# Moving a cross-attention layer's key and value projections one layer earlier, through device memory

## The chip, the cores and the metric

The kernel runs on one core of a Trainium2 chip. The metric is the device time of one execution in microseconds (us). Before the change it is 2668.98 us, the median of three runs (2668.42 to 2671.52).

The core's engines work side by side: TensorE (PE) multiplies matrices out of the on-chip memory into eight accumulation banks, VectorE (DVE), ScalarE (ACT) and GpSimd (POOL) do elementwise work, and SyncE (SP) issues all the transfers of this kernel. [...]

## The reference, cut to what matters

Four attention layers run one after the other on 16 sequences of 128 rows by 512 columns. `ctx` is a second input of the same shape that no layer changes.

```python
x = L0(ctx, x, mask)          # latent attention, then an MLP
x = L1(x, ctx, mask)          # grouped attention (32 query heads, 8 key heads), no MLP
x = L2(x, ctx, mask)          # cross attention (16 heads), then an MLP
x = L3(ctx, x, mask)          # latent attention, then an MLP

def L1(hidden, enc, mask):
    q, k, v = hidden @ Wq + bq, enc @ Wk + bk, enc @ Wv + bv
    x = attention(q, k, v) @ Wo + bo + hidden
    return normalized(x) * gamma + beta

def L2(hidden, enc, mask):
    q = layer_norm(hidden) @ q_w + q_b
    k, v = enc @ k_w + k_b, enc @ v_w + v_b      # enc is ctx: they depend on no earlier layer
    hidden = attention(q, k, v) @ cproj_w + cproj_b + hidden
    return hidden + mlp(layer_norm(hidden))
```

## The kernel before

All four layers work on pairs of sequences, `p` from 0 to 7. Each matrix product is made in three passes (`three_passes`, L317): every operand is split into a rounded part and the rest, and high times high, high times low and low times high are summed. `ctx` is split once, in layer 0, and kept in device memory as `ctx_split`. Each later layer loads one pair of it (1 MB, `sp_c`, L1444) into the first half of each block of `XC`; the second half gets the layer's own input, turned by PE (`pe_turn_x`, L350) and split by ACT and DVE (`act_x`, `dve_x`). Weights come in 256 KB tiles: SP loads one into one of two buffers (`load_tile`, L296) and POOL splits it (`split_tile`, L304 to L308). SP loads tile n only when tile n-2 is split.

A pair runs in rounds: four in the grouped layer, two in the cross layer. A round is a chain. PE makes the scores (L317 with 32 rows), DVE takes the maxima (grouped: fused with the addition of the mask, L950; cross: L954), ACT the exponentials (L700), DVE the inverse sums (L972), POOL scales (`pool_norm`, L1274), PE turns the result (L453), ACT and DVE copy it out (L684, L959), and PE multiplies it with the values (`pe_attend`, L480). PE makes the scores of round k+1 before it turns round k. ACT and DVE then take the heads out (L714, L999), and after a sequence's last round comes the output projection (`pe_out`). DVE adds the residual (L1093) and takes the moments (L1078 to L1087), and POOL normalizes (`pool_root`, L1302 to L1309; in the grouped layer a second time for the next layer, `pool_again`, L1315). Scores, and the MLP's sums, use four of the eight banks. All other products share a ring of the other four (`begin`): a product can start when the bank used four products ago has been emptied.

The projections for pair p+1 stand between the rounds of pair p. In the grouped layer these are one small key block, two query blocks and one value block. In the cross layer they are two key blocks (`pe_keys`), two query blocks and two value blocks (`pe_values`); each key or query block is 24 matmuls of 256 columns, each value block 12 of 512. Keys and values go to `KT_C` and `V_C` by ACT (L730, L684) and DVE (L1017, L959), queries to `QT` (L738, L1026). Keys and queries stand together, after the first `pe_attend` of the pair, and the first key block waits until `dve_x` is done with pair p+1 (`aff_split`), although only the queries need it. The cross layer's 16 weight tiles are split by POOL in the grouped layer, two in each pair. The order on each engine is written out by hand in the functions named after it (`pe_gqa`, `act_gqa`, `dve_gqa`, `pool_gqa`, `sp_gqa` and so on for `cross`).

## Time and profile before

| | before |
|---|---|
| median of three runs | 2668.98 us |
| profiled execution | 2673.65 us, its span 2671.9 us |
| PE busy over the span | 93% (weight loads 78%) |
| DVE, ACT, POOL busy over the span | 46%, 41%, 41% |
| grouped layer, first key block to first cross projection | 802.45 to 1190.11 us |
| cross layer, from there to the first MLP product | 1190.11 to 1522.67 us |
| mean granted PE clock of the core | 0.97 of full |

A busy share over the whole span hides that the stages have different limits: in the MLPs PE never stops, in the grouped layer POOL is the busiest engine. The profiled execution is 4.7 us above the median of the three runs. [...]

### The profile page before, as it was taken

Reading aid. Unit: us, or ns where it says so; the run is one execution under the profiler, and the core shown is the slowest. Engines: PE = TensorE matmul, PEld = TensorE weight load, DVE = VectorE, ACT = ScalarE, POOL = GpSimd, SP = SyncE. Lnnn points to the kernel's source line nnn. Section 1 sums busy time; section 2 is a strip of 40 time slices with the busy share of each in tenths; the row PEclk is TensorE's granted clock in tenths of the full one; section 3 lists DMA queues with packets and bytes.
Section 4 is the critical chain, followed back from the end, with each engine's and each line's share of the span. In section 5 each row is a group of like instructions: output and inputs, shape, how many; then the busy total and the mean of one; then the engine's idle time right before and its main releaser. Section 6 shows DMA issues by size and latency. Waiting matters only on the chain.

```text
span 2671.9 us, 48698 instructions
## 1 busy us (share of the span) xinstructions
PE 2474.4 (93%) x18464; PEld 2072.0 (78%) x18464; DVE 1230.2 (46%) x3295; ACT 1086.5 (41%) x3705; POOL 1105.6 (41%) x1972
## 2 busy tenths in 40 slices
PE   7999998999997788857988899999899999899999
PEld 5887886888886666747877788888788888688887
DVE  4555564323225766644445533332355555432322
ACT  4555563111117777745556411111355555311111
POOL 2454446400035898963544560003244444640000
PEclk9999999999999999978999999999899999999999
DMA  4112212211112222221222231112211211321100
GB/s 155 57 57 70 90 49 92 63 48 48 56 61 85 82 92 83 66 84 64 72 96 92 76 122 48 48 40 61 78 49 49 89 48 49 98 63 41 48 32 16
DMA packets 110326, 181.30 MB, mean 68 GB/s; under 512 B 7888, under 2 KB 43408, under 8 KB 109072
## 3 DMA queue, kind: packets, MB, share of 16 engines
q1 hardware_dynamic: 110096, 178.19, 20.3%
q8 instruction: 149, 2.44, 0.4%
q14 instruction: 81, 0.66, 0.1%
HBM read 132.02 MB, written 46.14 MB: 67 GB/s over the span
## 4 chain that ended last, share of the span: by engine, by line
PE 80%; POOL 7%; ACT 6%; DVE 4%; issue 2%; DMA 1%; SPq 0%; DVEq 0%; POOLq 0%; ACTq 0%
PE banks L317 71%; PE banks L453 5%; ACT plain_high L700 4%; POOL plain_high L1274 4%; PE banks L480 3%; DVE neg_max L954 1%; PE banks L504 1%; DVE rounded_work L1052 1%; DVE plain_high L950 0%; POOL rounded_high L308 0%; POOL rounded_low L308 0%; PE banks L442 0%; DVE rounded_work L1026 0%; POOL rstd L1289 0%; ACT plain_high L684 0%
## 5 line engine op out<-in xcount | busy, mean ns | idle before, releaser
L317 PE MATMUL banks<-rounded_work,rounded_low 128*128 128x512 f32 (+1 forms) x2688 | 535.2, 357 | 58.3 <-issue 35.3
L1274 POOL TENSOR_SCALAR plain_high<-plain_high,inv_sum 128x128 f32<-128x128 f32 (+1 forms) x1024 | 386.7, 401 | 392.4 <-DVE inv_sum L972 391.3
L317 PEld LDWEIGHTS banks<-rounded_work,rounded_low 128*128 128x128 f32 x2688 | 447.4, 200 | 125.4 <-issue 53.6
L317 PE MATMUL banks<-rounded_work,rounded_high 128*128 128x512 f32 (+1 forms) x2400 | 488.2, 357 | 8.6 <-DMA rounded_work<-ctx_split 6.4
L929 ACT ACTIVATE plain_work<-banks,columns 128x512 f32<-128x512 f32 x192 | 132.5, 690 | 865.2 <-PE banks L317 865.2
L317 PEld LDWEIGHTS banks<-rounded_work,rounded_high 128*128 128x128 f32 x2400 | 399.1, 192 | 76.6 <-issue 9.4
L1250 DVE CAST rounded_work<-plain_work 128x512 fp32r<-128x512 f32 x192 | 102.0, 531 | 689.3 <-ACT plain_work L929 678.1
L317 PE MATMUL banks<-rounded_low,rounded_work 128*128 128x512 f32 x1728 | 413.1, 391 | 0.0
L317 PE MATMUL banks<-rounded_high,rounded_work 128*128 128x512 f32 (+1 forms) x1728 | 395.2, 381 | 0.0
L317 PEld LDWEIGHTS banks<-rounded_low,rounded_work 128*128 128x128 f32 x1728 | 322.1, 188 | 69.0 <-issue 3.0
L317 PEld LDWEIGHTS banks<-rounded_high,rounded_work 128*128 128x128 f32 x1728 | 314.1, 192 | 60.5 <-issue 1.4
L1412 POOL TENSOR_TENSOR plain_work<-plain_work 128x512 f32<-128x512 f32 x48 | 66.5, 1416 | 608.0 <-DMA plain_work<-x 417.4
L453 PE MATMUL banks<-ident,plain_high 128*128 128x128 f32 x1280 | 182.0, 289 | 59.8 <-POOL plain_high L1274 42.4
L700 ACT ACTIVATE plain_high<-plain_high,neg_max 128x128 f32<-128x128 f32 x512 | 198.0, 391 | 47.6 <-DVE neg_max L950 47.6
L954 DVE TENSOR_REDUCE neg_max<-banks 128x2 f32<-128x512 f32 (+1 forms) x320 | 204.5, 681 | 24.4 <-PE banks L442 24.4
L1274 POOL TENSOR_SCALAR plain_low<-plain_low,inv_sum 128x256 f32<-128x256 f32 x256 | 117.1, 479 | 237.4 <-DVE inv_sum L972 237.4
L453 PEld LDWEIGHTS banks<-ident,plain_high 128*128 128x128 f32 x1280 | 144.0, 146 | 90.2 <-issue 53.0
L700 ACT ACTIVATE plain_high<-banks,neg_max 128x256 f32<-128x256 f32 (+1 forms) x512 | 209.5, 462 | 7.4 <-DVE neg_max L954 7.4
L1252 DVE TENSOR_TENSOR rounded_work<-plain_work,rounded_work 128x512 fp32r<-128x512 f32 x192 | 159.1, 829 | 6.6
L972 DVE RECIPROCAL inv_sum<-row_sum 128x4 f32<-128x4 f32 (+1 forms) x224 | 41.4, 186 | 212.0 <-ACT plain_high L700 168.9
L317 PEld LDWEIGHTS banks<-rounded_work 32*128 32x128 f32 x3072 | 101.6, 188 | 43.0 <-issue 40.7
L317 PE MATMUL banks<-rounded_work 32*128 32x256 f32 (+1 forms) x3072 | 123.5, 292 | 10.2 <-DVE rounded_work L1026 8.1
(101 smaller groups left out, 3058.0 us busy)
## 6 DMA issues: line engine op xcount, KB each, us to landing
plain_work<-x SPq DMA_DIRECT2D x96, 256.0 KB, 2.8
plain_work<-mlp_w SPq DMA_DIRECT2D x96, 256.0 KB, 2.7
rounded_work<-ctx_split SPq DMA_DIRECT2D x24, 1024.0 KB, 5.9
u<-plain_work SPq DMA_DIRECT2D x48, 256.0 KB, 3.0
plain_work<-u SPq DMA_DIRECT2D x12, 1024.0 KB, 7.2
x<-plain_work SPq DMA_DIRECT2D x48, 256.0 KB, 2.2
plain_work<-attention_w SPq DMA_DIRECT2D x44, 256.0 KB, 2.7
plain_work<-inputs_t SPq DMA_DIRECT2D x8, 1024.0 KB, 7.8
```

What stands on the lines that cost most here:

```text
L317: mm = pe.matmul(dst, lhs(i), rhs(j), start=first and n == 0, stop=last and n == 2, skip_group_check=True)
L453: mm = pe.transpose(dst[:, t * P:(t + 1) * P], pr[:, r, t * P:(t + 1) * P], ident[:, :])
L480: mm = pe.matmul(dst[32 * r:32 * r + 32, i * P:(i + 1) * P], v, pt[:, r, at:at + P], start=t == 0, stop=t == n_t - 1, skip_group_check=True)
L504: mm = pe.transpose(dst[:, r * P:(r + 1) * P], u_nat[:, r, f * P:(f + 1) * P], ident[:, :])
L700: last = act.activation(pr[:, r, part], pr[:, r, part] if gqa else PS[:, r, part], ACT.Exp, scale=-1.0 if gqa else 1.0, bias=neg_max[:, R ...
L929: act.activation(gelu[:, j % 2, :], bank(key), ACT.Gelu_apprx_tanh, bias=col(y, 28 + j)).then_inc(evac_of(key), 1)
L954: dve.tensor_reduce(neg_max[:, R % 2, r, 0:y.segs], src.rearrange("p (g n) -> p g n", g=y.segs), AX.X, ALU.max, negate=True).then_inc(maxe ...
L972: dve.reciprocal(inv_sum[:, R % 2, 2 * half:2 * half + 2, 0:y.segs], row_sum[:, R % 2, 2 * half:2 * half + 2, 0:y.segs]).then_inc(inverted, 1)
L1250: dve.tensor_copy(G[:, j % 4, 0, :], gelu[:, j % 2, :]).then_inc(g_hi, 1)
L1252: dve.tensor_tensor(G[:, j % 4, 1, :], gelu[:, j % 2, :], G[:, j % 4, 0, :].bitcast(F32), ALU.subtract).then_inc(g_ready, 1)
L1274: last = pool.tensor_scalar(part, part, inv_sum[:, R % 2, r, g:g + 1], 1.0, ALU.mult, ALU.mult)
L1412: last = pool.tensor_tensor(res[:, r, :], res[:, r, :], wide_bias, ALU.add)
```

## The change

The cross layer's key and value projections move into the grouped layer. While `XC` holds the `ctx` half of pair p+1 for the grouped layer's own keys, PE also makes the two key and two value blocks of the cross layer from it. ACT and DVE put them into new buffers `k_ahead` and `v_ahead` (one of each), SP stores them in device memory (1 MB of keys and 512 KB of values for each pair), and the cross layer loads them back into two `KT_C` and two `V_C` buffers. The cross layer no longer loads `ctx_split`. Its input has its own buffer `XT_C`.

- PE, grouped layer: all four blocks of pair 0 stand ahead of the second scores. For each later pair, a key block stands after the first `pe_attend`, a key block after the second, a value block after the third and a value block at the end of the pair. Cross layer: keys and values are gone, and `pe_out` of the pair before moves from behind the queries to a place ahead of the first `pe_attend`; DVE's `dve_out` moves likewise.
- ACT and DVE follow. ACT waits for the stored keys or values of the pair before ahead of the next evacuation.
- SP: `ctx_split` for the grouped layer's pair p+1 is loaded when the cross layer's last value block of pair p is done (before: when the grouped layer's value block of pair p was). Key and value stores are added, and for pair 0 both stand ahead of the load for pair 1.
- POOL: of the cross layer's 16 tiles, the eight of keys and values are split in the last stretch of layer 0's MLP; four query tiles in pairs 0 to 3 of the grouped layer; four output tiles at the start of the cross layer.

PE in the grouped layer, before: one whole pair, from its second scores (L317 at 128x256 x24 from `rounded_work` alone; L453 turns, L350 turns the input, L480 attends, other L317 rows are projections).

```order
L317 MATMUL banks<-rounded_work 128x256 x24
L453 MATMUL banks<-ident,plain_high 128x128 x16
L350 MATMUL banks<-ident,plain_work 128x128 x8
L317 MATMUL banks<-rounded_high 128x512 x12
L480 MATMUL banks<-plain_work 32x128 x16
L317 MATMUL banks<-rounded_work,rounded_high 128x256 x12
L317 MATMUL banks<-rounded_work 128x256 x24
L453 MATMUL banks<-ident,plain_high 128x128 x16
L317 MATMUL banks<-rounded_work,rounded_high 128x256 x24
L480 MATMUL banks<-plain_work 32x128 x16
L317 MATMUL banks<-rounded_work 128x256 x24
```

The same stretch after the change:

```order
L324 MATMUL banks<-rounded_work 128x256 x24
L465 MATMUL banks<-ident,plain_high 128x128 x16
L359 MATMUL banks<-ident,plain_work 128x128 x8
L324 MATMUL banks<-rounded_high 128x512 x12
L495 MATMUL banks<-plain_work 32x128 x16
L324 MATMUL banks<-rounded_work,rounded_high 128x256 x12
L324 MATMUL banks<-rounded_work,rounded_low 128x256 x24
L324 MATMUL banks<-rounded_work 128x256 x24
L465 MATMUL banks<-ident,plain_high 128x128 x16
L324 MATMUL banks<-rounded_work,rounded_high 128x256 x24
L495 MATMUL banks<-plain_work 32x128 x16
L324 MATMUL banks<-rounded_work,rounded_low 128x256 x24
```

The two new rows `rounded_work,rounded_low 128x256 x24` are the cross layer's key blocks, each between an attend and the next scores.

PE in the cross layer, before: from a pair's second scores to those of the next pair.

```order
L317 MATMUL banks<-rounded_work 128x128 x48
L442 MATMUL banks<-plain_work,ones_row 128x512 x4
L453 MATMUL banks<-ident,plain_high 128x128 x16
L350 MATMUL banks<-ident,plain_work 128x128 x8
L480 MATMUL banks<-plain_high,plain_work 32x128 x16
L317 MATMUL banks<-rounded_work,rounded_low 128x256 x96
L317 MATMUL banks<-rounded_low,rounded_high 128x512 x12
L317 MATMUL banks<-rounded_work 128x128 x48
L442 MATMUL banks<-plain_work,ones_row 128x512 x4
L453 MATMUL banks<-ident,plain_high 128x128 x16
L317 MATMUL banks<-rounded_low,rounded_high 128x512 x12
L480 MATMUL banks<-plain_high,plain_work 32x128 x16
```

After:

```order
L324 MATMUL banks<-rounded_work 128x128 x48
L454 MATMUL banks<-plain_work,ones_row 128x512 x4
L465 MATMUL banks<-ident,plain_high 128x128 x16
L359 MATMUL banks<-ident,plain_work 128x128 x8
L324 MATMUL banks<-rounded_low,rounded_high 128x512 x12
L495 MATMUL banks<-plain_high,plain_work 32x128 x16
L324 MATMUL banks<-rounded_work,rounded_low 128x256 x48
L324 MATMUL banks<-rounded_work 128x128 x48
L454 MATMUL banks<-plain_work,ones_row 128x512 x4
L465 MATMUL banks<-ident,plain_high 128x128 x16
L324 MATMUL banks<-rounded_low,rounded_high 128x512 x12
L495 MATMUL banks<-plain_high,plain_work 32x128 x16
```

The 96 projection matmuls have become 48, the two value blocks that followed the last row are gone, and an output projection has moved from behind the queries to the place ahead of the attend.

The diff, cut to its core:

```diff
--- before.py
+++ after.py
-        KT_C = work(rounded, 16, 2, 4, 2 * P)
+        KT_C = [work(rounded, 16 - 8 * h, 2, 4, 2 * P) for h in range(2)]
+        XT_C = work(rounded, 0, 2, FB, 2 * P)
+        k_ahead, v_ahead = slots(rounded, 6, 2, 4, 2 * P), slots(plain, 7, 2, D)
...
         def pe_keys(pe, y, p, i):
-            if i == 0:
+            if i == 0 and y.kind != CROSS:
...
             if p == 0:
                 pe_weights(pe, y, "q")
+            if y.kind == CROSS and i == 0:
+                pe_inputs(pe, y, p)
+            x_t = XT_C if y.kind == CROSS else XC[:, :, :, 2 * P:4 * P]
...
+                pe.wait_ge(kt_loaded[p % 2], 16 * (p // 2 + 1))
                 for i in range(2):
-                    wait_evac(pe, ("K", y.n, p, i))
                     wait_evac(pe, ("Q", y.n, p, i))
...
+            if y.kind == CROSS:
+                pe.wait_ge(vc_loaded[p % 2], 16 * (p // 2 + 1))
...
             pe_scores(pe, y, 0, 0)
             pe_queries(pe, y, 0, 1)
             pe_values(pe, y, 0, 0)
+            for i in range(2):
+                pe_keys(pe, L[2], 0, i)
+            for i in range(2):
+                pe_values(pe, L[2], 0, i)
...
                 if more:
                     pe_keys(pe, y, p + 1, 0)
+                    pe_keys(pe, L[2], p + 1, 0)
                 pe_scores(pe, y, p, 2)
                 pe_turn_probs(pe, y, p, 1)
                 if more:
                     pe_queries(pe, y, p + 1, 0)
                 pe_attend(pe, y, p, 1)
+                if more:
+                    pe_keys(pe, L[2], p + 1, 1)
                 pe_scores(pe, y, p, 3)
                 pe_turn_probs(pe, y, p, 2)
                 if more:
                     pe_values(pe, y, p + 1, 0)
                 pe_attend(pe, y, p, 2)
                 if more:
+                    pe_values(pe, L[2], p + 1, 0)
                     pe_scores(pe, y, p + 1, 0)
                 pe_turn_probs(pe, y, p, 3)
                 pe_out(pe, y, 2 * p)
                 pe_attend(pe, y, p, 3)
                 if more:
                     pe_queries(pe, y, p + 1, 1)
+                    pe_values(pe, L[2], p + 1, 1)
             pe_out(pe, y, B - 1)
 
         def pe_cross(pe, y):
             pe_turn_x(pe, y, 0)
             for i in range(2):
-                pe_keys(pe, y, 0, i)
-            for i in range(2):
                 pe_queries(pe, y, 0, i)
             pe_scores(pe, y, 0, 0)
-            for i in range(2):
-                pe_values(pe, y, 0, i)
...
                     pe_turn_x(pe, y, p + 1)
+                if p:
+                    pe_out(pe, y, 2 * p - 1)
                 pe_attend(pe, y, p, 0)
                 if more:
-                    for i in range(2):
-                        pe_keys(pe, y, p + 1, i)
                     for i in range(2):
                         pe_queries(pe, y, p + 1, i)
                 else:
                     for f in range(FB):
                         pe_turn_u(pe, M[y.n], 0, f)
-                if p:
-                    pe_out(pe, y, 2 * p - 1)
                 if more:
                     pe_scores(pe, y, p + 1, 0)
                 pe_turn_probs(pe, y, p, 1)
                 pe_out(pe, y, 2 * p)
                 pe_attend(pe, y, p, 1)
-                if more:
-                    for i in range(2):
-                        pe_values(pe, y, p + 1, i)
             pe_out(pe, y, B - 1)
...
+                if p and i == 0:
+                    act.wait_ge(k_stored, 16 * p)
                 for j in range(2):
                     t = 2 * i + j
-                    last = act.activation(KT_C[:, 0, t, :], bank(key)[:, j * 256:j * 256 + 256], ACT.Identity, bias=col(y, 4 + t))
+                    last = act.activation(k_ahead[:, 0, t, :], bank(key)[:, j * 256:j * 256 + 256], ACT.Identity, bias=col(y, 4 + t))
                 last.then_inc(hi_done, hi_count(key))
 
...
+                if y.kind == CROSS:
+                    wait(act, v_stored, 16 * p)
+                act_copy(act, key, v_ahead[:, i, :] if y.kind == CROSS else V_L[p % 2][:, i, :])
 
...
-                split_tile(pool, ("a", 2), 2 * p)
+                if p < 4:
+                    split_tile(pool, ("qo", 2), p)
                 pool_norm(pool, y, p, 3)
-                split_tile(pool, ("a", 2), 2 * p + 1)
                 pool_bias(pool, y, 2 * p + 1)
...
         def pool_cross(pool, y):
+            pool.wait_ge(k_stored, 16 * PAIRS)
+            pool.wait_ge(v_stored, 16 * PAIRS)
+            split_tile(pool, ("qo", 2), 4)
+            split_tile(pool, ("qo", 2), 5)
             pool_norm(pool, y, 0, 0)
+            split_tile(pool, ("qo", 2), 6)
+            split_tile(pool, ("qo", 2), 7)
...
+                pool.wait_ge(down_done, base + 8)
+                for i in range(8):
+                    split_tile(pool, ("kv", 2), i)
                 pool.wait_ge(down_done, base + 11)
-                for i in range(8, 12):
-                    split_tile(pool, ("a", 1), i)
+                for i in range(4):
+                    split_tile(pool, ("o", 1), i)
...
+        def sp_keys_ahead(sp, p):
+            for i in range(2):
+                wait_evac(sp, ("K", 2, p, i))
+            sp.dma_start(keys_of[p], k_ahead.rearrange("p a b c -> p (a b c)").bitcast(F32)).then_inc(k_stored, 16)
+
+        def sp_values_ahead(sp, p):
+            for i in range(2):
+                wait_evac(sp, ("V", 2, p, i))
+            sp.dma_start(values_of[p], v_ahead.rearrange("p a b -> p (a b)")).then_inc(v_stored, 16)
+
+        def sp_ahead(sp, p):
+            sp_keys_ahead(sp, p)
+            sp_values_ahead(sp, p)
+
+        def sp_cross_keys(sp, p):
+            sp.dma_start(KT_C[p % 2].rearrange("p a b c -> p (a b c)").bitcast(F32), keys_of[p]).then_inc(kt_loaded[p % 2], 16)
+
+        def sp_cross_values(sp, p):
+            sp.dma_start(V_C[p % 2].rearrange("p a b -> p (a b)"), values_of[p]).then_inc(vc_loaded[p % 2], 16)
+
         def sp_gqa(sp, y):
             sp.wait_ge(s_filled[3], M[0].u0 + GROUPS)
...
+            sp_ahead(sp, 0)
             for p in range(PAIRS):
                 more, far = p + 1 < PAIRS, p + 2 < PAIRS
                 if more:
-                    wait_filled(sp, v_last(y, p))
+                    wait_filled(sp, ("V", 2, p, 1))
                     sp_c(sp, y, p + 1)
                     if p:
                         sp.wait_ge(s_free[3], y.use(p - 1, 3) + 1)
                     sp_qk_mask(sp, p + 1)
-                load_tile(sp, ("a", 2), 2 * p)
-                load_tile(sp, ("a", 2), 2 * p + 1)
+                if p < 4:
+                    load_tile(sp, ("qo", 2), p)
                 if p:
+                    sp_values_ahead(sp, p)
                     sp_store_h(sp, y, 2 * p - 2)
                 if far:
                     wait_filled(sp, ("X", y.n, p + 1, 1))
...
                     sp_store_h(sp, y, 2 * p - 1)
                     sp_store_u(sp, y, 2 * p - 1)
                     sp_next_hidden(sp, y, 2 * p + 1)
+                if more:
+                    sp_keys_ahead(sp, p + 1)
...
-            wait_filled(sp, ("Q", 1, PAIRS - 1, 1))
-            sp_c(sp, y, 0)
+            wait_filled(sp, ("V", 2, PAIRS - 1, 1))
             sp_x(sp, y, 0)
+            sp.wait_ge(k_stored, 16 * PAIRS)
+            sp.wait_ge(v_stored, 16 * PAIRS)
+            load_tile(sp, ("qo", 2), 4)
+            load_tile(sp, ("qo", 2), 5)
             sp_mask(sp, y, 0)
+            sp.wait_ge(s_filled[3], prev.use(PAIRS - 1, 3) + 1)
+            sp_cross_keys(sp, 0)
+            sp_cross_keys(sp, 1)
+            wait_filled(sp, ("O", prev.round(PAIRS - 1, 3)))
+            sp_cross_values(sp, 0)
+            sp_cross_values(sp, 1)
             sp.wait_ge(biased, prev.b0 + B)
             sp_wide(sp, "L2_xattn_cproj_b")
             sp_gqa_tail(sp, prev)
...
-                if more:
-                    wait_filled(sp, v_last(y, p))
-                    sp_c(sp, y, p + 1)
+                if p and more:
+                    sp.wait_ge(s_filled[3], y.use(p - 1, 1) + 1)
+                    sp_cross_keys(sp, p + 1)
+                    wait_filled(sp, ("O", y.round(p - 1, 1)))
+                    sp_cross_values(sp, p + 1)
```

## Rows read from the trace of the kernel before

**Rows 1.** Stretches of six grouped and six cross pairs: from:to, length, each engine's busy time, clock, DMA.
```profile
859.55:1129.63 270.08, 219.87 (x2429) 183.99 (x2425) 186.67 (x1068) 211.57 (x930) 240.94 (x517) 0.94 0.25 80
1254.87:1495.36 240.49, 212.18 (x2114) 188.85 (x2113) 121.44 (x288) 132.81 (x558) 113.42 (x254) 0.92 0.27 91
```

**Rows 2.** Timeline of PE, grouped layer: start us, length us, engine, line, operation [idle before].
```profile
816.92 1.00 PE L317 MATMUL banks<-rounded_work 32*128 32x256 f32 x24
...
859.55 3.14 PE L317 MATMUL banks<-rounded_work,rounded_high 128*128 128x256 f32 x24
862.62 1.00 PE L317 MATMUL banks<-rounded_work 32*128 32x256 f32 x24
...
996.12 1.00 PE L317 MATMUL banks<-rounded_work 32*128 32x256 f32 x24
...
1005.05 1.69 PE L317 MATMUL banks<-rounded_work,rounded_high 128*128 128x256 f32 x12
...
1034.68 4.36 PE L317 MATMUL banks<-rounded_high 128*128 128x512 f32 x12
...
1129.56 3.13 PE L317 MATMUL banks<-rounded_work,rounded_high 128*128 128x256 f32 x24
```

**Rows 3.** Timeline of POOL, grouped layer: first and last scaling of a run of three.
```profile
1004.53 5.57 POOL L1274 TENSOR_SCALAR plain_high<-plain_high,inv_sum 128x128 f32<-128x128 f32 x16 [2.69 <-DVE inv_sum L972]
...
1028.22 5.57 POOL L1274 TENSOR_SCALAR plain_high<-plain_high,inv_sum 128x128 f32<-128x128 f32 x16
```

**Rows 4.** Timeline of PE, cross layer: its first block, then one pair and a later value block.
```profile
1190.11 13.72 PE L317 MATMUL banks<-rounded_work,rounded_low 128*128 128x256 f32 x96 [11.08 <-issue]
1205.88 1.59 PE L317 MATMUL banks<-rounded_work 32*128 32x128 f32 x48 [2.04 <-DVE rounded_work L1026]
...
1289.06 5.73 PE L317 MATMUL banks<-rounded_low,rounded_work 128*128 128x512 f32 x24
1294.72 1.58 PE L317 MATMUL banks<-rounded_work 32*128 32x128 f32 x48
...
1305.10 14.19 PE L317 MATMUL banks<-rounded_work,rounded_low 128*128 128x256 f32 x96 [3.44 <-issue]
...
1489.70 5.73 PE L317 MATMUL banks<-rounded_low,rounded_work 128*128 128x512 f32 x24
```

**Rows 5.** Timeline of ACT, cross layer: evacuations of the first two key blocks.
```profile
1195.24 0.84 ACT L730 ACTIVATE rounded_work<-banks,columns 128x256 fp32r<-128x256 f32 x2 [13.71 <-PE banks L317]
1198.11 0.84 ACT L730 ACTIVATE rounded_work<-banks,columns 128x256 fp32r<-128x256 f32 x2 [2.03 <-PE banks L317]
```

**Rows 6.** Timeline of DVE, cross layer: maxima, inverse sums, heads, the split of the input.
```profile
1283.54 1.28 DVE L954 TENSOR_REDUCE neg_max<-banks 128x4 f32<-128x512 f32 x2
...
1290.83 0.20 DVE L972 RECIPROCAL inv_sum<-row_sum 128x8 f32<-128x8 f32 x1 [2.58 <-ACT plain_high L700]
...
1292.74 1.12 DVE L999 SCALAR_TENSOR_TENSOR rounded_high<-banks,columns,rounded_high 128x128 fp32r<-128x128 f32 x4
...
1296.54 1.29 DVE L954 TENSOR_REDUCE neg_max<-banks 128x4 f32<-128x512 f32 x2 [1.02 <-PE banks L442]
...
1304.31 0.69 DVE L1043 TENSOR_TENSOR rounded_work<-plain_work,rounded_work 128x512 fp32r<-128x512 f32 x1
```

**Rows 7.** Transfers of the six grouped pairs: issuing engine, count, KB each, us to landing.
```profile
rounded_work<-ctx_split SPq DMA_DIRECT2D x5, 1024.0 KB, 5.9
x<-plain_work SPq DMA_DIRECT2D x12, 256.0 KB, 2.2
```

**Rows 8.** Timeline, end of layer 0's MLP: POOL's first, ninth and last splits; SP's load.
```profile
736.47 0.40 POOL L306 CAST rounded_high<-plain_work 128x256 fp32r<-128x256 f32 x1 [6.79 <-PE banks L317]
...
779.99 0.61 POOL L306 CAST rounded_high<-plain_work 128x512 fp32r<-128x512 f32 x1 [24.79 <-PE banks L317]
...
787.37 1.28 POOL L308 TENSOR_TENSOR rounded_high<-plain_work,rounded_high 128x512 fp32r<-128x512 f32 x1
```
```profile
793.55 0.61 SPq L1444 DMA_DIRECT2D rounded_work<-ctx_split x1
```

95 lines of the change are left out of this document (54 added, 41 removed).

## Prediction

> **What bounds the kernel now.** I read the busy shares first, then the same by stage, then the timelines of the two layers that the change touches, and last the chain of waits through them. The page's 93% for PE is a mean over stages. In the MLPs it is 100%, and there the change alters nothing. In the two attention layers it is not [rows 1]: over six grouped pairs PE is busy 219.87 of 270.08 us, POOL 240.94; over six cross pairs PE is busy 212.18 of 240.49 us and no other engine more than 133. So the grouped layer hangs on POOL and has PE time to spare, and the cross layer hangs on PE.
>
> Grouped layer: query blocks of the same kind start at 859.55 and, six pairs later, at 1129.56 [rows 2], so a pair takes 45.0 us. The chain through it is POOL's: the scaling that starts at 1004.53 and the one that ends at 1033.8 enclose 29.3 us in which POOL hardly stops (scalings, normalizations, one tile's split) [rows 3]. The remaining 15.7 us go through PE's last turn, output projection, attend and second query block, then through evacuation, maxima and exponentials back to POOL.
>
> Cross layer: value blocks start at 1289.06 and, five pairs later, at 1489.70 [rows 4], so a pair takes 40.1 us. PE stands still for 3.44 us in each pair ahead of the 96 projection matmuls, because the keys wait with the queries for the split input, and hardly elsewhere.
>
> **What moves, block by block.** Two key blocks are evacuated 2.88 us apart at full clock [rows 5]; two value blocks take 5.66 us from their start to the next scores [rows 4]. Four blocks are 5.75 + 5.66 = 11.4 us of PE per pair, taken from the cross layer and given to the grouped one.
>
> **Grouped layer, pairs 1 to 6.** PE is busy 36.65 us per pair now, in part at half clock (1034.68: 12 matmuls in 4.36 us [rows 2]; the granted clock over the stretch is 0.94 [rows 1]). With 11.4 us more it is 48.05 us, above today's 45.0: PE becomes the bound, and I take 48.1 us. A second way gives the same. Laying the new row of work out at full clock gives 43.7 us of PE; three of the four blocks stand directly ahead of scores and delay a round's maxima, and the waits for turned or scaled rows that are left come to about 4.5 us. The ends: 45.0 if every block falls into a gap that POOL leaves, 56.4 if none does. POOL itself loses work: two tiles per pair become one in pairs 0 to 3 and none later. One split lies on its chain, 2.2 us by the last four at the end of the MLP (779.99 to 788.65 [rows 8]), but this frees nothing once PE is last. ACT gets 2.3 us and DVE 2.4 us more per pair, on 35 and 31 us busy of 45; that is room enough, except that each key block is evacuated ahead of the next maxima (0.9 us of delay per round, in the 48.1). Six pairs at +3.1: **+18.5 us** (0 to +68).
>
> **Grouped layer, pair 0 and pair 7.** All four blocks stand ahead of the second scores, today at 816.92 [rows 2], with nothing to overlap but exponentials of the first round: +11.4. The rest of that pair takes 45.7 us without any finishing work on POOL (816.92 to the like scores at 862.62 [rows 2]); its rounds are bound by latency, and I add 1 us. Then a transfer: for pair 0 SP issues both stores ahead of `ctx_split` for pair 1. 1 MB lands in 5.9 us, 256 KB in 2.2 [rows 7], so each further 256 KB costs 1.2 and the 1.5 MB ahead 7.4 us. Landing would be 1.0 (evacuation) + 7.4 + 5.9 = 14.3 us after the second scores start, and the keys of pair 1 want it after 8.9 us (996.12 to 1005.05 in a later pair [rows 2]). That is 5 us of waiting (0 if transfers share the engines freely: they are 25% busy [rows 1]); I take **+5**. In later pairs only the load itself comes later: it is issued at the pair's start instead of a round earlier, and lands 5.9 to 6.9 us into a pair whose keys begin at 8.9; hidden, with 2 us to spare. Pair 7 has no added work and one split less on the chain: -2. Together **+15.4 us**.
>
> **Between the stages.** At the end of layer 0's MLP POOL has eight more tiles. Its last split ends at 788.65 today and SP's load of `ctx_split` is issued at 793.55 [rows 8], when the last hidden block is done. The gates of the first eight and of the last four tiles, eight steps of the MLP apart, open at 736.4 and 779.9, so a step is 5.44 us. The key and value tiles' gate, five steps after the first, opens at 763.6; eight tiles take 17.3 us at 2.17 each, and the last four end at 789.6: hidden, with 4 us to spare. If they were late, SP's load behind them would be too, by as much. The PE pause of 11.08 us ahead of the cross layer [rows 4] stays: it comes from the last normalizations on POOL and DVE, which do not change. Key and value loads for pairs 0 and 1 go out in the last round of the grouped layer and land 25 us before use; the four late output tiles are split while POOL would wait. All this at 0.
>
> **Cross layer.** Without key blocks the first scores come 5.75 us earlier. In each pair the bound is now a loop through all engines; I add its rows. From a pair's second maxima (1296.54) to the end of the input's split (1305.00) and PE's start at 1305.10: 8.56 [rows 4, 6]. Two query blocks: 5.75 at full clock; but the first block after a pause ran at half, 5.1 us (1190.11 to 1195.24 [rows 4, 5]), which would make 8.0; I take 6.9, since the moved output projection shortens the pause ahead to some 1.7 us. Evacuation to scores: 2.04 [rows 4], hidden today behind an output projection and bare from now on. Scores to maxima: 1294.72 to 1296.54, 1.82 [rows 4, 6]. Maxima to inverse sums, residual and moments, heads: 1283.54 to 1293.86, 10.3 [rows 6]; then come the next second maxima. The sum is 29.6 us against 40.1; PE's own work in it is only 22.6. Seven such steps: 7 x 10.5 = 73.5, with the first scores **-79.3 us** (28.4 to 30.7 per pair: -87 to -71). Key and value loads (1.5 MB per pair, instead of 1 MB) are issued about half a pair ahead and stay hidden.
>
> **The sum:** 18.5 + 15.4 - 79.3 = -45.4 us on the profiled execution's own 2673.65, so 2628; that execution lies 4.7 above the median, which gives 2624 us.
>
> **Rivals.**
> *Half clock in the cross layer (0.06).* PE would work 22.6 of 29.6 us, less densely than today. The clock is 0.92 there now and falls after each 3.44 us pause. If both query blocks (5.1 each) and the scores ran at half, a pair would cost 3.3 + 1.2 more: 7 x 4.5 = 31, giving 2655 us. Against it: the grouped layer, with PE at 81%, holds 0.94 [rows 1]. [...]
>
> *Nothing hidden in the grouped layer (0.03), the slower side.* The rounds there are already bound by latency where POOL is free (45.7 us in pair 0). If each block is added in full and one per pair runs at half clock (+2.2), a pair costs 13.6 more instead of 3.1: +63 us, 2687 us. It turns the sign from 10.7 exposed us per pair on. Against it: PE is idle or at half clock for more than 10 of 45 us there.
>
> *Late keys in the cross layer (0.03).* SP issues the loads behind stores that wait for POOL's normalizations. 6.5 us of waiting per pair would undo the gain: 29.6 + 6.5 = 36.1, 7 x 4.0 + 5.75 against 33.9, no change, 2669. So would any other reason why a cross pair stays near 36. Against it: two buffers and half a pair of lead.
>
> *The grouped layer swallows the blocks (0.07).* A pair stays at 45.0 and the wait in pair 0 does not appear: -23.5 more, 2600 us.
>
> **Chances.** The forecast has 0.81. Its own range is 46.5 to 50.5 per grouped pair (-10, +14) and 28.4 to 30.7 per cross pair (-8, +8): 2605 to 2645. To hold 8 in 10 with the last rival and half of the spread between forecast and first rival, I give 2598 to 2650; what is left out is 0.06 + 0.03 + 0.03 and a little at the lower end. A measurement of this kernel tells 0.2% (5.3 us) from no change. Faster by more: 0.81 + 0.06 + 0.07 = 0.94; within: 0.03; slower: 0.03.
>
> **What would show it.** In the new profile, like rows one pair apart in the grouped layer should be 48 us apart, PE's busy share there 95% or more, and POOL's waits longer. The cross layer's should be 29 to 30 apart, with pauses ahead of the queries and of the scores behind them. The first key block of pair 1 should wait some 5 us for a DMA. A granted clock under 0.85 in the cross layer speaks for the first rival, a grouped pair above 52 us for the second, DMA named ahead of cross scores for the third.

## The result, and the profile after

| | median | runs | profiled execution |
|---|---|---|---|
| before | 2670.25 us | 2668.42 to 2674.08 (4) | span 2671.9 |
| after | 2628.38 us | 2625.52 to 2633.31 (4) | 2633.31, span 2631.4 |

The ratio is 0.984, with a 95% interval of 0.982 to 0.987: 42 us less, a change clear of the spread of the runs though under 2%. The forecast was 2624.0 us, 4.4 us too low, within its range of 2598 to 2650.

The same two stretches as [rows 1], after the change: six grouped pairs, then six cross pairs (span, then busy us of PE, PE's weight loads, DVE, ACT and POOL, granted clock, DMA share, GB/s).

```profile
872.65:1163.16 290.51, 270.63 (x2861) 235.78 (x2857) 200.57 (x1098) 225.60 (x961) 226.69 (x502) 0.98 0.30 103
1255.31:1434.30 178.99, 152.76 (x1680) 131.27 (x1680) 104.39 (x254) 120.23 (x531) 113.74 (x253) 0.90 0.38 129
```

The granted clock is the share of full speed that the profile shows for PE in a stretch. Full clock here is 1.00, as over the query blocks at 1315.30 below; half clock is 0.50, as over the turns at 1296.28 below, and in the kernel before over the first 3.9 us of the key blocks at 1190.11.

In the grouped layer PE went from 219.87 of 270.08 us to 270.63 of 290.51 (93%), and POOL fell below it (240.94 to 226.69). In the cross layer PE is busy 85% of a pair of 29.8 us instead of 40.1. The page's chain that ended last shows the same; before it read PE 80%, POOL 7%, ACT 6%, DVE 4%:

```profile
PE 77%; ACT 10%; DVE 7%; POOL 3%; issue 2%; DMA 1%; SPq 0%; DVEq 0%; POOLq 0%; ACTq 0%
```

PE's timeline in the grouped layer, after: pair 0 with its four added blocks, and two query blocks one pair apart (answers to [rows 2]; L324 was L317). Below, SP's queue in pair 0.

```profile
817.46 5.97 PE L324 MATMUL banks<-rounded_work,rounded_low 128*128 128x256 f32 x48
823.27 5.63 PE L324 MATMUL banks<-rounded_low,rounded_work 128*128 128x512 f32 x24
828.83 0.99 PE L324 MATMUL banks<-rounded_work 32*128 32x256 f32 x24
...
836.72 2.91 PE L324 MATMUL banks<-rounded_work,rounded_high 128*128 128x256 f32 x12 [0.88 <-DMA rounded_work<-ctx_split]
...
920.35 3.13 PE L324 MATMUL banks<-rounded_work,rounded_high 128*128 128x256 f32 x24
...
968.05 3.13 PE L324 MATMUL banks<-rounded_work,rounded_high 128*128 128x256 f32 x24
```
```profile
825.45 0.33 SPq L1579 DMA_DIRECT2D cross_keys<-rounded_low  x1
829.77 0.33 SPq L1584 DMA_DIRECT2D cross_values<-plain_low  x1
830.15 0.55 SPq L1477 DMA_DIRECT2D rounded_work<-ctx_split  x1
```

The four blocks take 828.83 - 817.46 = 11.4 us, a pair at full clock 968.05 - 920.35 = 47.7. The load waited for behind the stores costs 0.88 us.

PE's timeline in the cross layer, after (answers to [rows 4]), and DVE's in the same pair (answers to [rows 6]).

```profile
1224.49 8.10 PE L324 MATMUL banks<-rounded_work,rounded_low 128*128 128x256 f32 x48 [11.13 <-issue]
1234.63 1.58 PE L324 MATMUL banks<-rounded_work 32*128 32x128 f32 x48 [2.04 <-DVE rounded_work L1046]
...
1293.54 2.35 PE L324 MATMUL banks<-rounded_work 32*128 32x128 f32 x48 [2.04 <-DVE rounded_work L1046]
...
1296.28 3.67 PE L465 MATMUL banks<-ident,plain_high 128*128 128x128 f32 x16
...
1315.30 6.00 PE L324 MATMUL banks<-rounded_work,rounded_low 128*128 128x256 f32 x48 [1.30 <-DVE rounded_work L1066]
1323.34 1.59 PE L324 MATMUL banks<-rounded_work 32*128 32x128 f32 x48 [2.04 <-DVE rounded_work L1046]
```
```profile
1325.23 1.29 DVE L974 TENSOR_REDUCE neg_max<-banks 128x4 f32<-128x512 f32 x2 [2.14 <-PE banks L454]
...
1336.12 1.27 DVE L974 TENSOR_REDUCE neg_max<-banks 128x4 f32<-128x512 f32 x2
...
1343.52 0.69 DVE L1066 TENSOR_TENSOR rounded_work<-plain_work,rounded_work 128x512 fp32r<-128x512 f32 x1
```

The pause of 3.44 us ahead of the projections is now 1.30, and a gap of 2.04 us (the queries' evacuation) stands bare ahead of the scores. Behind it the next turns run partly or wholly at half clock in all seven pairs (2.79 to 3.67 us instead of 1.97).

### The profile page after: what moved, and what is told of

Same layout as the page of the kernel before. It is cut to its first block, busy times and chain, and to the rows that moved or that the text cites. A ratio compares the mean times of both kernels' runs of the same rounds, so it can differ in the third digit from the quotient of the medians.

```text
span 2631.4 us, 48760 instructions
## 1 busy us (share of the span) xinstructions
PE 2473.8 (94%) x18464; PEld 2073.3 (79%) x18464; DVE 1224.5 (47%) x3295; ACT 1088.4 (41%) x3705; POOL 1114.7 (42%) x1972
## 4 chain that ended last, share of the span: by engine, by line
PE 77%; ACT 10%; DVE 7%; POOL 3%; issue 2%; DMA 1%; SPq 0%; DVEq 0%; POOLq 0%; ACTq 0%
PE banks L324 69%; ACT plain_high L715 7%; PE banks L465 4%; PE banks L495 3%; DVE plain_high L970 1%; POOL plain_high L1298 1%; ACT plain_high L699 1%; ACT plain_work L780 1%; DVE stats L1101 1%; PE banks L519 1%; DVE rounded_work L1075 1%; DVE rounded_high L1019 1%; DMA rounded_work<-ctx_split 0%; POOL rounded_high L315 0%; DVE plain_work L1116 0%
## 5 line engine op out<-in xcount | busy, mean ns | idle before, releaser
L324 PE MATMUL banks<-rounded_work,rounded_low 128*128 128x512 f32 (+1 forms) x2688 | 526.0, 350 | 45.2 <-DVE rounded_low L1130 13.7
L324 PEld LDWEIGHTS banks<-rounded_work,rounded_low 128*128 128x128 f32 x2688 | 435.6, 193 | 114.1 <-issue 29.2
L324 PE MATMUL banks<-rounded_work,rounded_high 128*128 128x512 f32 (+1 forms) x2400 | 487.6, 357 | 7.4 <-DMA rounded_work<-ctx_split 7.1
L324 PEld LDWEIGHTS banks<-rounded_work,rounded_high 128*128 128x128 f32 x2400 | 398.1, 192 | 75.7 <-DMA rounded_work<-ctx_split 7.7
L324 PE MATMUL banks<-rounded_low,rounded_work 128*128 128x512 f32 x1728 | 418.2, 394 | 0.0
L324 PE MATMUL banks<-rounded_high,rounded_work 128*128 128x512 f32 (+1 forms) x1728 | 390.2, 377 | 0.0
L324 PEld LDWEIGHTS banks<-rounded_low,rounded_work 128*128 128x128 f32 x1728 | 324.6, 190 | 69.9 <-issue 3.3
L324 PEld LDWEIGHTS banks<-rounded_high,rounded_work 128*128 128x128 f32 x1728 | 309.1, 188 | 60.6 <-issue 1.4
L715 ACT ACTIVATE plain_high<-plain_high,neg_max 128x128 f32<-128x128 f32 x512 | 197.8, 391 | 17.5 <-DVE neg_max L970 17.5
L465 PEld LDWEIGHTS banks<-ident,plain_high 128*128 128x128 f32 x1280 | 154.0, 152 | 33.6 <-issue 18.4
L324 PE MATMUL banks<-rounded_work 32*128 32x256 f32 (+1 forms) x3072 | 132.4, 299 | 27.0 <-DVE rounded_work L1046 20.3
L324 PEld LDWEIGHTS banks<-rounded_work 32*128 32x128 f32 x3072 | 109.6, 194 | 60.7 <-issue 55.4
```

Of the source, the lines that this page charges most:

```text
L324: mm = pe.matmul(dst, lhs(i), rhs(j), start=first and n == 0, stop=last and n == 2, skip_group_check=True)
L465: mm = pe.transpose(dst[:, t * P:(t + 1) * P], pr[:, r, t * P:(t + 1) * P], ident[:, :])
L715: last = act.activation(pr[:, r, part], pr[:, r, part] if gqa else PS[:, r, part], ACT.Exp, scale=-1.0 if gqa else 1.0, bias=neg_max[:, R ...
```

## Experiments

Theory: the blocks cost little in the grouped layer, where PE had time to spare, and leave a cross layer that is no longer bound by PE but by a loop through all engines. Rivals: the gain is the removed pause and not the removed work; POOL's relief matters; the moved output projection matters. The four runs of the changed kernel lie between 2625.5 and 2633.3 us, so a difference of less than about 5 us between two medians says little by itself. Its profiled execution was its slowest one: the grouped layer, from first turn of the input to that of the cross layer, took 415.6 us there and 411.6 to 412.0 in the profiles of "output back", "warm" and "last pair", whose grouped layers are the same. The pair times below run between first turns of the input: five grouped pairs (before: 865.36 to 1091.01, 45.1 us each) and six cross pairs (before: 1217.88 to 1458.49, 40.1).

| kernel | median us | ratio to before (95%) | grouped pair | cross pair |
|---|---|---|---|---|
| before | 2670 | | 45.1 | 40.1 |
| after | 2628.4 | 0.984 (0.982 to 0.987) | 48.6 | 29.5 |
| no blocks (one run) | 2604.5 | | 45.7 | 29.4 |
| keys free (from before) | 2628.6 | 0.984 (0.983 to 0.986) | 45.1 | 34.6 |
| keys free, output moved | 2648.1 | 0.991 (0.990 to 0.993) | 44.9 | 37.2 |
| output back | 2633.0 | 0.986 (0.985 to 0.988) | 48.5 | 30.7 |
| warm | 2619.8 | 0.981 (0.980 to 0.982) | 48.3 | 28.7 |
| x early | 2618.6 | 0.980 (0.979 to 0.982) | 48.5 | 27.9 |
| one value block home | 2614.7 | 0.980 (0.978 to 0.981) | 47.2 | 29.4 |
| both value blocks home | 2610.9 | 0.978 (0.976 to 0.979) | 45.9 | 30.1 |
| last pair | 2622.4 | 0.982 (0.980 to 0.983) | 48.3 | 29.0 |
| pause | 2621.7 | 0.982 (0.980 to 0.983) | 48.9 | 29.7 |
| four edits in one | 2602.7 | 0.975 (0.973 to 0.976) | 46.4 | 30.0 |

### What the blocks cost in the grouped layer

```diff
                 if more:
                     pe_keys(pe, y, p + 1, 0)
-                    pe_keys(pe, L[2], p + 1, 0)
...
-                if more:
-                    pe_keys(pe, L[2], p + 1, 1)
...
-                    pe_values(pe, L[2], p + 1, 0)
...
-                    pe_values(pe, L[2], p + 1, 1)
```

> The changed kernel without the cross layer's key and value blocks of pairs 1 to 7 in the grouped layer (their matmuls, evacuations and waits are left out; the stores and loads stay and carry pair 0's data, so the cross layer's output is not the reference's). Theory A (TensorE sets the grouped pair in the changed kernel, 47.7 us, and the grouped pair without the blocks is set by a chain through GpSimd's scaling that takes about 45 us as before): a clean pair falls by 47.7 - 45.0 = 2.7 us to about 45, not by the blocks' 11.4, so that 8.7 us of the blocks' work per pair lay in idle time of TensorE. Theory B (fewer tile splits on GpSimd have shortened that chain): 42 to 43 us per pair. Theory C (the blocks lie on the path in full): 47.7 - 11.4 = 36.3 us.

This kernel leaves out work that the cross layer needs, so only its times are read. A pair of it, then one of the changed kernel at full clock and one that is partly at half:

```profile
913.18:958.46 45.28, 38.38 (x408) 32.46 (x404) 30.20 (x176) 34.02 (x148) 36.65 (x80) 0.89 0.33 115
```
```profile
920.35:968.05 47.70, 44.44 (x481) 38.71 (x477) 33.43 (x183) 37.62 (x161) 39.07 (x86) 1.00 0.31 109
1024.26:1074.77 50.51, 47.14 (x478) 40.92 (x477) 33.43 (x186) 37.59 (x161) 36.54 (x83) 0.93 0.29 98
```

45.28 us: theory A. Of 11.4 us of blocks per pair 2.4 show (2.9 in the mean of five pairs), in part because the clock rises from 0.89 to 1.00: PE's busy time grows by 6.1 us only. Fewer splits on POOL haven't shortened these pairs (45.7 us against 45.1 before). Pair 7 alone seems to gain: from its turn of the input to that of the cross layer this kernel takes 84.95 us and the kernel before 86.99. That is all that POOL's relief can have brought. The third row shows what sets the pair now. In the changed kernel half clock adds 2.7 us to PE's busy time and 2.8 to the pair. Without the blocks half clock doesn't show: pairs with PE busy for 37.2 and 38.4 us both take 45.3.

### Is it the work or the pause?

The kernel before, with one wait in another place:

```diff
             pe.wait_ge(c_loaded, 16 * (c_index(y, p) + 1))
-            if y.kind == CROSS:
-                pe.wait_ge(aff_split, 2 * p + 2)
-            else:
+            if y.kind != CROSS:
...
                 pe_weights(pe, y, "q")
+            if y.kind == CROSS and i == 0:
+                pe.wait_ge(aff_split, 2 * p + 2)
```

> The kernel before with one edit in the cross layer: the key blocks of the next pair wait only for their context, and the wait for the split queries' input (aff_split) stands at the first query block. Nothing is moved between layers. Theory A (what the change bought in the cross layer is 10.4 us of TensorE work per pair, and the 3.44 us pause with the half clock behind it is only part of it): the pause goes and the blocks behind it run at full clock, 3.44 + about 2.2 = 5.6 us per pair, 7 x 5.6 = 39 us less, 2631 us, as fast as the changed kernel although it moves nothing; then most of the changed kernel's gain could have been had without the move. Theory B (closing this pause only opens the next one, at the query block, since the split input comes no earlier): about half of it, 7 x 2.8 = 20 us less, 2650 us. Theory C (the pause costs nothing, the cross layer is set by other engines): 2670 us.

Five cross pairs of the kernel before, and five of this one:

```profile
1258.42:1458.49 200.07, 176.47 (x1762) 157.03 (x1761) 101.20 (x241) 110.67 (x467) 98.09 (x216) 0.92 0.27 91
```
```profile
1248.40:1420.49 172.09, 165.66 (x1763) 146.43 (x1762) 101.25 (x241) 109.86 (x467) 99.00 (x216) 1.00 0.32 106
```

Theory A. A pair falls from 40.0 to 34.4 us. Of the 5.6 us that it saves, (176.47 - 165.66) / 5 = 2.2 are busy time that ran at half clock before, 3.4 are the pause. PE is now 96% busy. The same wait also held pair 0's keys, which now fill half of the 11.08 us pause ahead of the layer: 34.6 us from its first turn to the next instead of 39.9. So a kernel that moves one wait is as fast as the changed kernel (2628.6 and 2628.4 us), with nothing stored. The move of work takes more out of the cross layer (29.5 instead of 34.6 per pair) and pays about as much in the grouped one (+33.7 us, see below).

The same with the output projection moved as in the changed kernel:

```diff
+                if p:
+                    pe_out(pe, y, 2 * p - 1)
                 pe_attend(pe, y, p, 0)
...
                         pe_turn_u(pe, M[y.n], 0, f)
-                if p:
-                    pe_out(pe, y, 2 * p - 1)
```

> As the run with the free key blocks, and in addition the output block of the odd sample, out(2p-1), stands before the first attend on TensorE and before its heads on VectorE, as in the changed kernel. Theory A (TensorE's work sets the pair once the pause is gone; the output block between queries and scores covers the 2 us in which the queries are evacuated, and moving it away uncovers them): 7 x (0 to 2) = 0 to 14 us more than the run with the free key blocks alone. Theory B (the move is itself a gain, since VectorE then takes the maxima of the next scores 2 us earlier): 7 x 2 = 14 us less than that run.

```profile
1267.52 1.59 PE L317 MATMUL banks<-rounded_work 32*128 32x128 f32 x48 [2.04 <-DVE rounded_work L1026]
1268.89 0.45 PE L442 MATMUL banks<-plain_work,ones_row 32*128 32x512 bf16 x4
1269.27 3.22 PE L453 MATMUL banks<-ident,plain_high 128*128 128x128 f32 x16
```

19.5 us slower, 2.6 us per pair: the 2.04 us that the block had covered lie bare, and the turns behind them run in part at half clock. With PE 96% busy, what filled the gap was worth more than what it delayed on DVE. Theory A had the sign and ended at 14 us. It left the clock out: over five pairs PE's busy time grows from 165.66 to 174.80 us at a clock of 0.95 instead of 1.00.

### What closes the loop in the cross layer

The changed kernel with the output projection in its old place (the edit above, turned round, with DVE's `dve_out`):

> The changed kernel with out(2p-1) back between the queries and the next scores, on TensorE and on VectorE. Theory A (the loop of the cross layer runs through VectorE and ScalarE, and the output block in it adds its 2.83 us and VectorE's 2 us, less the 2.04 us gap that it fills): 2 to 3 us more per pair, 7 x 2.4 = 17 us more than the changed kernel, 2645 us. Theory B (the query blocks start when the split input is there, whatever stands before; the output block fills the 2.04 us gap and adds only 0.8): 7 x 0.8 = 6 us more, 2634 us. Theory C (the filled gap keeps the full clock and wins it back): 2628 us or less.

2633.0 us, 4.6 more, with intervals that overlap; the cross pair is 1.2 us longer, near theory B's 0.8. In the profiles six pairs grow from 177.2 to 184.2 us, while the grouped layer, which this edit doesn't touch, took 3.9 us less. So the moved block is worth some 7 us in the cross layer, and the medians alone don't settle it. Most of the gain isn't there.

ScalarE's two affine steps for the next input, ahead of the second exponential:

```diff
+            if y.kind == CROSS:
+                between()
             if k is not None:
                 act_exp(act, y, p, k, 1)
-            between()
+            if y.kind != CROSS:
+                between()
```

> The changed kernel; on ScalarE the two affine steps of the next queries' input (act_x) stand ahead of the second exponential of the round instead of behind it, in the cross layer alone. Theory A (the cross pair of the changed kernel is a loop in which the queries wait for the split input, 1.28 us of gap before the query blocks, and ScalarE's order sets that gap): the gap closes, 7 x 1.3 = 9 us less than the changed kernel, 2619 us. Theory B (the exponentials are in the loop too, and taking their turn later costs what is won): 2628 us. Theory C (the next scores wait longer for the freed banks): up to 1 us per pair more, 2635 us.

PE's timeline around the query blocks of a pair:

```profile
1281.17 1.08 PE L495 MATMUL banks<-plain_high,plain_work 128*32 128x128 f32 x32
1282.18 6.01 PE L324 MATMUL banks<-rounded_work,rounded_low 128*128 128x256 f32 x48
```

No gap is left ahead of the queries. A cross pair falls by 1.7 us, the kernel by 9.8: theory A. The intervals don't overlap. ACT's order is in the loop, although ACT is busy only 67% of the changed kernel's pair.

Idle matmuls in the two gaps:

```diff
                 if more:
+                    fill_gap(pe, y, 4)
                     for i in range(2):
                         pe_queries(pe, y, p + 1, i)
+                    fill_gap(pe, y, 8)
```

> The changed kernel with idle work for TensorE in the two gaps of the cross layer's loop: 4 matmuls of 128x512 before the queries (about 0.95 us in a gap of 1.28) and 8 behind them (1.9 us in a gap of 2.04), into the next free bank, which is overwritten. Theory A (the half clock right behind the 2.04 us gap costs time: turns of 3.4 instead of 2.2 us): 1.2 us less per pair, 7 x 1.2 = 8 us less than the changed kernel, 2620 us, with the granted clock of the cross layer at 0.97 or more instead of 0.90. Theory B (the loop is closed by the other engines and slow turns are hidden): 2628 us with a higher clock. Theory C (the added matmuls delay the queries or the scores): up to 7 x 1 = 7 us more.

```profile
1286.58 2.00 PE L625 MATMUL banks<-rounded_low 128*128 128x512 f32 x8
1288.79 1.59 PE L324 MATMUL banks<-rounded_work 32*128 32x128 f32 x48 [0.21 <-DVE rounded_work L1056]
...
1290.54 1.97 PE L465 MATMUL banks<-ident,plain_high 128*128 128x128 f32 x16
```

2619.8 us, 8.6 less: theory A's size. The intervals just touch, and only some 5 us of it lie in the six cross pairs of the profiles (177.2 to 172.3 us); 3.6 lie in the grouped layer, which the edit doesn't touch. Turns behind the filled gap take 1.97 us in all seven pairs instead of 2.79 to 3.67. The granted clock over six pairs went to 0.95, not to 0.97: in five of seven pairs the second turns took 2.94 to 3.68 us and not 2.22. So half clock costs the changed kernel at least 0.8 us per cross pair; how much of the rest of the 29.5 it explains isn't shown.

### How much should move?

V(p+1,1) back in the cross layer, its context loaded once more:

```diff
                     for i in range(2):
                         pe_queries(pe, y, p + 1, i)
+                    pe_values(pe, y, p + 1, 1)
```

> The changed kernel with one of the four blocks of each pair back in the cross layer: the values of the odd sample, V(p+1,1), computed behind the queries, in the 2.04 us gap before the scores; its context is loaded again (1 MB per pair, into the slots of the key weights). Three blocks stay in the grouped layer. Theory A (the grouped pair is bound by TensorE down to about 45 us, and the cross pair by a loop with a gap that hides the block): grouped 47.7 - 2.7 = 45.0 us per pair, 6 x 2.7 + 2.8 = 19 us less; cross 2.83 - 2.04 = +0.8 us and about -1.2 us for the clock that stays up, nothing; 2609 us. Theory B (the block adds its full 2.83 us to the loop of the cross layer, VectorE's copy included): 7 x 2.83 = 20 us given back, 2628 us.

Both value blocks back, one ahead of the queries and one behind:

```diff
+                    pe_values(pe, y, p + 1, 0)
                     for i in range(2):
                         pe_queries(pe, y, p + 1, i)
+                    pe_values(pe, y, p + 1, 1)
```

> As the run with one block back, with both value blocks of each pair in the cross layer: V(p+1,0) before the queries (gap 1.28 us) and V(p+1,1) behind them (gap 2.04 us); only the keys are computed in the grouped layer, and no values are stored. Theory A: grouped pair at its floor of about 45 us, 6 x 2.7 + 5.7 = 22 us less than the changed kernel; cross (2.83 - 1.28) + (2.83 - 2.04) - 1.2 = +1.1 us per pair, 8 us more; 2614 us. Theory B (both blocks add in full to the loop): 7 x 5.7 = 40 us given back, 2646 us. Theory C (the grouped floor has sunk too, since GpSimd splits fewer tiles there than before): 43 us per pair, 12 us less again, 2602 us.

Two grouped pairs and two cross pairs of the kernel with both back:

```profile
916.32:962.92 46.60, 40.40 (x454) 35.31 (x453) 32.63 (x183) 37.22 (x160) 39.95 (x87) 0.96 0.30 101
962.92:1008.46 45.54, 40.36 (x455) 35.66 (x454) 32.65 (x183) 37.23 (x160) 38.05 (x85) 0.96 0.30 97
```
```profile
1341.11:1401.81 60.70, 57.24 (x610) 48.39 (x609) 36.60 (x89) 41.00 (x179) 39.12 (x87) 1.00 0.43 149
```

One block back gives 13.6 us, both give 17.5; the 3.9 between them are within the spread of the runs. In the grouped layer a pair takes 45.7 us with none of the blocks, 45.9 with two (46.4 in the last run below), 47.2 with three and 48.6 with four (48.3 to 48.9 in all kernels that have four). The first two are nearly free, each further one costs about 1.4. In the cross layer a pair takes 29.5 with no value block and 30.1 with both, 5.7 us of work for 0.6. They fill the two gaps, and the clock is 1.00 in the two pairs shown and 0.97 over six, with PE 95% busy. Moving the keys alone beats moving nothing: 2610.9 us against the 2628.6 of the kernel with free keys, 17.7 less, though the two also differ in where the output projection stands. Moving the values as well gives that back. For one block theory A had 19 us and got 13.6, because the grouped pair came down to 47.2 only and not to 45. For both, 2610.9 lies 3 us below theory A's 2614.

### The ends of the cross layer

The last pair with out(13) behind the turns of `u`, as before:

> The changed kernel with the old order in the last pair of the cross layer alone: out(13) behind the four turn_u blocks on TensorE and VectorE. Theory A (the 3.5 us by which the stretch from the last scores to the MLP has grown come from turn_u waiting for VectorE's dve_out(13)): up to 3 us less than the changed kernel, 2625 us. Theory B (they come from the half clock and from other waits there): 2628 us.

Tail of the changed kernel, then of this one:

```profile
1462.67 0.66 PE L519 MATMUL banks<-ident,plain_work 128*128 128x128 f32 x4 [1.82 <-DVE plain_work L1116]
...
1477.74 4.61 PE L324 MATMUL banks<-rounded_low,rounded_high 128*128 128x512 f32 x12 [2.42 <-DVE rounded_high L1019]
1482.19 8.35 PE L324 MATMUL banks<-rounded_work,rounded_high 128*128 128x512 f32 x36
```
```profile
1452.41 1.99 PE L519 MATMUL banks<-ident,plain_work 128*128 128x128 f32 x12
...
1468.90 3.03 PE L324 MATMUL banks<-rounded_low,rounded_high 128*128 128x512 f32 x12 [2.42 <-DVE rounded_high L1021]
```

The wait of 1.82 us is gone and the last output projection runs at full clock. From the last turn of the input to the MLP the stretch is 2.3 us shorter (55.2 and 52.9). The median is 6.0 us lower, with intervals that overlap. In the profiles the rest isn't the edit's: the grouped layer took 3.6 us less, and the six cross pairs away from the edit 3.4 less at a clock of 0.93 instead of 0.90. The edit is worth 2.3 us; the share of half clock differs from one execution to the next (PE's mean clock was 0.970 to 0.973 in the changed kernel's four).

DVE's first mask and splits of the cross layer ahead of the last statistics of the grouped layer:

```diff
             dve_out(dve, y, B - 1)
+            dve_mask(dve, L[2], 0)
+            dve_x(dve, L[2], 0, 0)
+            dve_x(dve, L[2], 0, 1)
             dve_again(dve, y, B - 1)
```

> The changed kernel; on VectorE the first mask and the two splits of the cross layer's first input stand ahead of the last statistics of the grouped layer (dve_again of sample 15) instead of behind them. Nothing else. Theory A (the 11.1 us pause of TensorE before the cross layer's first blocks, which the change left as it was, comes from VectorE waiting 4.5 us for GpSimd's last normalisation with the splits queued behind): the queries start about 6 us earlier, 2622 us. Theory B (the pause has another release, the query weights or a load): 2628 us.

```profile
1211.24 1.04 PE L359 MATMUL banks<-ident,plain_work 128*128 128x128 f32 x8
1217.72 7.57 PE L324 MATMUL banks<-rounded_work,rounded_low 128*128 128x256 f32 x48 [5.44 <-issue]
```

DVE in the changed kernel, then the end of the early splits in this one:

```profile
1220.90 0.69 DVE L1101 BATCH_NORM_STATS2 stats<-plain_work 128x6 f32<-128x512 f32 x1 [4.51 <-POOL plain_work L1333]
...
1223.70 0.69 DVE L1066 TENSOR_TENSOR rounded_work<-plain_work,rounded_work 128x512 fp32r<-128x512 f32 x1
```
```profile
1216.92 0.69 DVE L1066 TENSOR_TENSOR rounded_work<-plain_work,rounded_work 128x512 fp32r<-128x512 f32 x1
```

The pause is 5.44 us instead of 11.13: theory A. The median is 6.7 us lower, with intervals that overlap; in the profiles the layer's first turn and the next lie 31.2 us apart instead of 37.4. This pause has nothing to do with the moved work: a finished transpose waited in DVE's queue behind a wait of 4.51 us for POOL.

Four edits in one kernel: both value blocks at home, the old last pair, the early splits, and pair 0's value blocks between the turns and the queries. ScalarE's earlier steps and the idle matmuls aren't in it.

> All that has paid so far in one kernel: both value blocks of each pair back in the cross layer, keys alone one layer earlier, the last pair in its old order, the first splits of the cross layer ahead of the last statistics, and pair 0's two value blocks between the turns of x and the queries, in the pause before them. Theory A (the gains are in different places and add): both values at home -17.5, last pair -3 to -6, splits earlier -6, two blocks of 5.7 us into the pause partly -3: 30 us less than the changed kernel, 2598 us. Theory B (the two edits of the pause take the same idle time, and the last pair's gain is the clock's and varies): -17.5 - 3 - 6 = 2602 us.

```profile
1191.12 1.03 PE L361 MATMUL banks<-ident,plain_work 128*128 128x128 f32 x8
1191.91 5.70 PE L326 MATMUL banks<-rounded_low 128*128 128x512 f32 x24
1197.62 5.98 PE L326 MATMUL banks<-rounded_work,rounded_low 128*128 128x256 f32 x48
1205.64 1.58 PE L326 MATMUL banks<-rounded_work 32*128 32x128 f32 x48 [2.04 <-DVE rounded_work L1051]
```

2602.7 us, 2.5% below the kernel before and 25.7 us below the changed one. It is theory B's number, not the full sum of 30. The pause is filled with work, and the queries run at full clock without a wait ahead of them; the 2.04 us ahead of the scores stay. Not run: the kernel with free keys and the early splits, with nothing moved. The kernel with free keys has 5.40 us left of that pause, so an estimate for it is 2623 us at best, still 20 above this one.

## Why the prediction was right

- **Block size.** 11.4 us for four, and 11.4 measured in pair 0.
- **Grouped pairs.** Predicted 48.1, measured 47.7 at full clock and 48.4 over six (290.51 / 6); +20.4 us instead of +18.5. That PE takes over from POOL is shown by the pairs in which half clock lengthens the pair by as much as PE's busy time; each further block adds 1.4 us and not its own 2.8, so the bound isn't PE's work alone. The first way, by the busy sum, hit by luck: it added full-clock blocks to half-clock work and no wait, but the clock rose to 0.98, and PE stands for 3.3 us per pair, mostly for the copies of turned rows. The second way had the mechanism: 43.7 us of work at full clock and 4.5 of waits, measured 44.4 and 3.3. PE's share came to 93%, not to the 95% named as a sign.
- **Pair 0 and pair 7.** The layer's growth of 33.7 us (1224.49 - 803.11 against 1190.11 - 802.45 at the like rows of before) leaves 13.3 for these, predicted 15.4. Cut at the scores that open pair 1 and pair 7, pair 0 grew by 15.2 us (878.46 - 803.11 against 862.62 - 802.45) and pair 7 by -2.0 (1224.49 - 1168.96 against 1190.11 - 1132.62), as predicted. In pair 0 the mis-sized terms are the transfer, 5 us predicted and 0.88 measured, and the rest of the pair, 1 us predicted and 2.9 measured (15.2 less 11.4 and 0.9). The transfer step counted 1.5 MB of stores as finished ahead of the load, at 1.2 us for each 256 KB. SP's rows show the keys' store 4.7 us and the values' store 0.4 us ahead of the load, and the load landed within 6.6 us of its issue, against 5.9 for the loads of other pairs. That is near the other end that the prediction named, no wait; what the stores did to the load isn't shown.
- **Pause before the cross layer.** Predicted unchanged, 11.08 and 11.13. The reason given, the last normalizations, holds (the pause run), but they held PE only through DVE's order.
- **First scores.** -5.75 predicted; 1234.63 - 1224.49 = 10.1 us against 15.8: -5.6.
- **The loop.** 29.6 predicted; 28.97 in the pair shown and 29.8 over the six from query block to query block (29.5 between turns). By its rows: maxima to maxima 1336.12 - 1325.23 = 10.9 (predicted 10.3), to the queries at 1344.27 8.15 (8.56), two query blocks 6.0 (6.9), evacuation 2.04 (2.04), scores to maxima 1.89 (1.82). Half clock was placed wrongly: I gave it to the query blocks behind the short pause, and it came to the scores and turns behind the 2.04 us gap, at about the same price; that the mean hits 29.6 is in part luck. Seven steps: 1451.41 - 1234.63 = 216.8 against 289.5: -72.7, predicted -73.5.
- **What was missing.** The tail. From the last scores to the MLP it takes 1482.19 - 1451.41 = 30.8 us against 27.3. The prediction moved the output projection in every pair and didn't ask what the last pair does: the turns of `u` need a bank that out(13), now ahead, still holds. +3.5 us, of which the run with the old last pair won back 2.3.
- **The sum.** 33.7 - 5.6 - 72.7 + 3.5 = -41.1; the spans differ by 40.5. The other 0.6 lie ahead of the grouped layer, which starts at 803.11 instead of 802.45. The forecast had -45.4, and the tail is most of the difference.
- **Rivals.** Half clock in the cross layer came in part: the clock is 0.90, below the 0.92 of before and above the 0.85 named as a sign, and filling the gaps won 0.8 us per pair, not 4.5. The clock does fall behind the recurring gaps of 2.04 us: the turns there took 2.79 to 3.67 us instead of 1.97. The query blocks behind each 1.3 us pause took 6.0 us, near full clock. No DMA is named ahead of cross scores. What the prediction didn't weigh at all is the cheapest alternative, the pause removed without the move, which gives the same time.

## What to carry to other kernels

Before work is moved out of a stage because an engine is full there, look at what its pauses cost in that stage: a wait that stands one block too early cost 3.4 us and 2.2 us of half clock per pair here. Moving that wait brought as much as moving all four blocks, and moving the keys alone brought 17.7 us more than that. Work moved into the grouped layer's idle time was nearly free up to its slack and then was not (45.7, 45.9, 47.2 and 48.6 us per pair with none, two, three and four blocks), so move in steps and stop where the receiver's pair begins to grow, and keep at home what fills a gap. At the end of the grouped layer DVE waited 4.51 us for POOL with finished input queued behind; taking that input first cut PE's pause from 11.13 to 5.44 us. Put what is ready ahead of such a wait.

## What the runs showed of the hardware

- With two value blocks of PE work in gaps of 1.3 and 2.04 us the granted clock was 1.00 over two cross pairs and 0.97 over six, with PE 94% and 95% busy; with the gaps open it was 0.90 at 85% busy.
- Removing one 3.44 us pause per pair brought the clock over five cross pairs from 0.92 to 1.00, and PE's busy time for the same matmuls (1762 and 1763 recorded) from 176.47 to 165.66 us. Behind the 3.44 us pauses the 96 projection matmuls took 13.1 to 14.5 us, without the pause 11.8.
- Query blocks behind a pause of 1.3 us took 6.0 us, near full clock. Behind the gap of 2.04 us in the same pairs the scores took 1.58 to 2.86 us and the turns 2.79 to 3.67, where full clock is 1.58 and 1.97. In the kernel with free keys and the output moved, three of its seven pairs had full-clock turns (1.97 us) behind the same gap. With both gaps filled the second turns, behind a wait of 0.85 us, still took 2.94 to 3.68 us in five of seven pairs and 2.22 in two. So the pause just ahead doesn't by itself decide the clock.
- A 1 MB load issued 0.4 us behind a 512 KB store and 4.7 us behind a 1 MB store landed after 6.5 us. The sixteen 1 MB loads of `ctx_split` that the kernel before issued for its grouped and cross layers took 5.5 to 7.1, so no price of the stores can be told.
